# Causal heads of a four-stage layer kernel: products with values in one batch per head instead of two, and 14 places for exponentials instead of 9

## The chip, the cores and the metric

The kernel runs on one core of one Trainium2 chip, as one launch. The metric is the device time of that launch in microseconds; lower is better. Before the change the median of three runs is 1224.54 us (1223.82 to 1226.81).

## The reference

The input `x` has 2 sequences of 1024 tokens with 128 values each. Four stages follow one another, each as `x = layernorm(x + stage(x))`:

```
L0 attention: q, k, v = x W.T + b; 16 heads of 8;  softmax(causal(q k.T / sqrt(8))) v;  W_o
L0 experts:   router, best 2 of 8, relu(x W1 + b1) W2 + b2, weighted sum
L1 attention: q, k through two low-rank factors; 16 heads of 8; causal softmax; W_o
L1 experts:   16 heads of 4 WITHOUT a causal mask, then a router, 8 experts with gelu
```

So there are three attentions. Each has 32 heads (16 heads times 2 sequences), 96 in all. Heads 0 to 31 and 32 to 63 are causal, heads 64 to 95 are not.

## The kernel before, in words

**Two runs.** `RUNS` has heads 0 to 31, followed by 32 units of expert work, and heads 32 to 95, followed by 32 units again. Every engine has its own written-out program over the same loops, and semaphores tie them. Nothing is planned at run time.

**A head.** The scores of a head are made twice. *By query* (`scores_by_query`, line 1195, into three PSUM banks `S1`): VectorE takes row maxima from them (`find_max`, lines 944 and 950). The negated maxima of a head are split in three bf16 parts by GpSimd (`split_max`), turned by TensorE (`max_rows`, line 1218), copied by ScalarE (`rows`, line 828) and sent by a DMA into spare rows of the head's keys and queries. *By key* (`scores_by_key`, line 1210, three PSUM banks `S2`): these come out with the maximum already taken off, and ScalarE writes their exponentials to `probs` (line 851). A causal head has 9 chunks of 512 columns of either sort, since the blocks above the diagonal are left out. Two of the 9 by-query chunks start with a mask product (line 1190); the exponentials of chunks 0 and 5 are masked by GpSimd (line 702). The by-query chunks run two heads ahead of the by-key ones: `head` on TensorE issues by-query chunk c+1 of head g+2 and then by-key chunk c of head g.

**Products with values.** `probs_by_v` (line 1239) multiplies the exponentials (fp32, in `probs`) with a head's values, which stand in 32 columns. A piece is one block of keys against 1 to 4 blocks of queries, and it writes one of four quarters of 32 partitions of the bank `SUM`. `by_key` gives each piece its quarter. Each piece is an fp32 product and shows in the trace as two records. A causal head has 18 pieces, so 36 records. They come in two batches. The batches are `range(0, 5)` and `range(5, 9)` of the chunks. In head g TensorE issues: five pairs of chunks, `max_rows(g + 1)`, **the second batch of head g-1**, a step of other work (`between(at_head(g, 0))`), four pairs of chunks, in every second head `turn_sums`, **the first batch of head g**, and another step of other work (`between(at_head(g, 1))`).

**Places of exponentials.** Chunk c of every causal head goes to place c of 9 in `probs`. ScalarE therefore waits with chunk c of head g until the batch of head g-1 that reads place c is done (`pv_before`, semaphore `pv`).

**A group.** Two causal heads share `SUM`. After the second, ScalarE copies it (`take_sums`, line 833), TensorE turns it (`turn_sums`, line 1249) into the bank `SHARED`, ScalarE takes it out (`take_out`, line 839), GpSimd adds the quarters, and VectorE divides (`normalise`, lines 965 and 967).

**The shared bank.** `SHARED` (bank 7) is used in turn by `max_rows`, `turn_sums` and the steps of other work: transposes, projections, router logits, queries, keys and values of the next attention (lines 1265 to 1327, 1161). `move_in` makes TensorE wait until the last tenant has been taken out. The list `BETWEEN` fixes by hand at which place (head, batch) each step stands. In the causal heads, the steps that use the bank stand after the first of TensorE's stretches, place (g, 0), at heads 13 to 16, 18, 23, 27, 28, 34, 35, 50, 51, 53, 54, 55 and 56. They stand after the second, place (g, 1), at heads 13 to 19, 22, 23, 27, 28, 33, 34, 49, 50, 53, 54, 55 and 56. At even heads `turn_sums` comes before (g, 1).

Of the kernel before, what the change touches and what calls it, by code (L numbers as in the profile page):

```python
# [13 lines left out]
P = 128  # L14
# [5 lines left out]
NH = B * H  # L20
# [3 lines left out]
CH = 512  # L24
# [6 lines left out]
RING = 4  # L31
# [10 lines left out]
class Attention:  # L42


    def __init__(self, layer, head_dim, scale_dim, causal):
        self.layer = layer
        self.hd = head_dim
        self.width = H * head_dim
        self.rows = PARTS * PARTS * head_dim
        self.dv = head_dim + 1  # L50
        self.group = 16 // head_dim
        self.scale = float(scale_dim) ** -0.5
        self.causal = causal
        if causal:

            diagonal = [[(i, i, 1) for i in range(4 * c, 4 * c + 4)] for c in range(2)]
            self.by_query = diagonal + [
                [(7, 0, 4)], [(7, 4, 3), (1, 0, 1)], [(6, 0, 4)], [(6, 4, 2), (2, 0, 2)],
                [(5, 0, 4)], [(5, 4, 1), (3, 0, 3)], [(4, 0, 4)]]
            self.maxima = 3  # L60

            self.by_key = [
                [(i, i, 1, 3) for i in range(4)], [(0, 4, 4, 0)], [(1, 4, 4, 1)], [(2, 4, 4, 2)],
# [3 lines left out]
            self.masked = (0, 5)  # L67
            self.batches = [range(0, 5), range(5, 9)]

            self.pv_order = [  # L70
                [(1, 0), (2, 0), (3, 0), (4, 0), (0, 0), (4, 1), (0, 1), (0, 2), (0, 3)],
                [(6, 0), (8, 0), (7, 0), (8, 1), (5, 1), (5, 0), (7, 1), (5, 2), (5, 3)]]
            self.adds = 3
        else:
            self.by_query = [[(i, 4 * c, 4)] for i in range(TB) for c in range(2)]
            self.maxima = 2
            self.by_key = [[(j, 4 * half, 4, 2 * half + j % 2)] for two in range(0, TB, 2) for half in range(2)
                           for j in range(two, two + 2)]
            self.masked = ()
            self.batches = [range(c, c + 4) for c in range(0, 16, 4)]  # L80
            self.pv_order = [[(c, 0) for c in batch] for batch in self.batches]
            self.adds = 1
        self.chunks = len(self.by_key)

# [7 lines left out]
class Head:  # L92
# [25 lines left out]
            self.key_rows = slice(64 * half, 64 * half + 64)  # L118
            self.max_row = 64 * half + QUERY_ROWS

    def batch_of(self, c):
        return next(k for k, batch in enumerate(self.a.batches) if c in batch)

    def probs_place(self, c):
        return c if self.a.causal else c % 8


HEADS = [Head(g) for g in range(3 * NH)]
RUNS = (range(0, NH), range(NH, 3 * NH))
CHUNKS = [sum(hd.a.chunks for hd in HEADS[:g]) for g in range(3 * NH + 1)]  # L130
BATCHES = [sum(len(hd.a.batches) for hd in HEADS[:g]) for g in range(3 * NH + 1)]
GROUP = [sum(hd.ends_group for hd in HEADS[:g]) for g in range(3 * NH + 1)]
GROUPS = [[hd for hd in HEADS if GROUP[hd.g] == i] for i in range(GROUP[-1])]
ADDS = [sum(heads[0].a.adds for heads in GROUPS[:i]) for i in range(len(GROUPS) + 1)]
# [2 lines left out]
def pv_before(g, c):  # L137

    if not HEADS[g].a.causal and c >= 8:
        return BATCHES[g] + (c - 8) // 4 + 1  # L140
    if g == 0:
        return 0
    if HEADS[g - 1].a.causal:
        return BATCHES[g - 1] + HEADS[g - 1].batch_of(c) + 1
    return BATCHES[g - 1] + (c + 8) // 4 + 1


def queries_upto(run, g, c):
# [172 lines left out]
def build(nc, inp, out):  # L321
    ctx = ExitStack()
    with ctx:
# [20 lines left out]
        qk = sb("qk", [P, RING, 2, S], BF16)  # L344
        v_all = [sb("v8", [P, NH, TB, 9]), sb("v4", [P, NH, TB, 5])]
        v_heads = [sb("v_head8", [P, RING, TB, Q]), sb("v_head4", [P, RING, TB, Q])]
        probs = sb("probs", [P, 9, CH])
        sums = sb("sums", [P, 2, CH])
        by_quarter = sb("by_quarter", [P, 2, 4, 4, 20])
        pairs = sb("pairs", [P, 4, 18])  # L350
# [220 lines left out]
        def _(pool):  # L571
# [81 lines left out]
            def take_v(g):  # L653
                hd = HEADS[g]
                a = hd.a
                ge(pool, "pv", BATCHES[max(g - RING + 1, 0)])
                if a.layer == 0 and hd.n == 0:
                    pool.wait_ge(sem("v_first"), NCH)
                if a.layer > 0 and hd.h == 0:
                    taken(pool, "v", a.layer, BY_SEQUENCE[hd.b][-1])  # L660
                at = a.dv * (hd.n % a.group)
                nc.gpsimd.tensor_copy(v_head_of(a)[:, hd.slot, :, at:at + a.dv], v_of(a)[:, hd.n, :, :]
                                      ).then_inc(sem("v_head"), 1)
# [73 lines left out]
        def _(act):  # L737
# [90 lines left out]
                nc.scalar.activation(neg_rows[:, g % RING, :], neg_ps, ACT.Copy).then_inc(sem("neg_rows"), 1)  # L828

            def take_sums(i):  # L830
                act.wait_ge(sem("pv"), BATCHES[GROUPS[i][-1].g + 1])
                ge(act, "out", i - 1)
                nc.scalar.activation(sums[:, i % 2, :], SUM[:], ACT.Copy).then_inc(sem("sums"), 1)

# [304 lines left out]
        def _(pe):  # L1139
# [81 lines left out]
            def probs_by_v(g, k):  # L1221
                hd = HEADS[g]
                a = hd.a
                order = [(c, b, a.by_key[c][b][1] // 4, a.by_key[c][b][3]) for batch in a.pv_order for c, b in batch]
                opens = {next(m for m in order if m[2:] == hq) for hq in {m[2:] for m in order}}
                closes = {next(m for m in reversed(order) if m[2:] == hq) for hq in {m[2:] for m in order}}
                if k == 0:
                    pe.wait_ge(sem("v_head"), g + 1)
                    if hd.first_of_group:
                        ge(pe, "sums", GROUP[g])  # L1230
                pe.wait_ge(sem("probs"), CHUNKS[g] + a.batches[k][-1] + 1)
                for c, b in a.pv_order[k]:
                    if c in a.masked and (c, b) == next(y for y in a.pv_order[k] if y[0] == c):
                        pe.wait_ge(sem("masked"), 2 * g + a.masked.index(c) + 1)
                    j, q0, count, quarter = a.by_key[c][b]
                    at = P * sum(blk[2] for blk in a.by_key[c][:b])
                    half, q = q0 // 4, P * (q0 % 4)
                    this = (c, b, half, quarter)
                    ins = mm(SUM[Q * quarter:Q * (quarter + 1), q:q + P * count], v_head_of(a)[:, hd.slot, j, :],  # L1239
                             probs[:, hd.probs_place(c), at:at + P * count],  # L1240
                             start=this in opens and hd.first_of_group, stop=this in closes and hd.ends_group,
                             skip_group_check=True)
                ins.then_inc(sem("pv"), 1)
# [87 lines left out]
            def head(run, g, asked):  # L1331
                hd = HEADS[g]
                for k, batch in enumerate(hd.a.batches):
# [11 lines left out]
                        max_rows(g + 1)  # L1345
                    if k == 1 and g > run.start and HEADS[g - 1].ends_group:
                        turn_sums(GROUP[g - 1])
                    if k > 0:
                        probs_by_v(g, k - 1)
                    elif g > run.start:  # L1350
                        probs_by_v(g - 1, len(HEADS[g - 1].a.batches) - 1)
                    if hd.a.causal:
                        between(at_head(g, k))
                return asked
# [35 lines left out]
            for f, run in enumerate(RUNS):  # L1390
# [9 lines left out]
                for g in run:  # L1400
                    asked = head(run, g, asked)
                last = run.stop - 1
                probs_by_v(last, len(HEADS[last].a.batches) - 1)
                experts(f, GROUP[last])


# [68 lines left out]
```

## Time and profile before

| | |
|---|---|
| median of 3 runs | 1224.54 us |
| profiled execution | 1223.02 us, its span 1221.2 us |
| causal heads | about 52 to 308 us and 460 to 735 us of the span |
| experts of the first run | about 308 to 460 us |
| heads 64 to 95 | about 735 to 995 us |
| mean granted TensorE clock | 0.986 of 2.4 GHz |

The page gives each engine's busy time, a strip of 40 slices of 30.5 us each (digits are tenths of busy time), the chain of waits that ended last, and groups of instructions by line. A timeline row gives the start, the time that a merged group covers, engine, line, tile names, shape of the first of them, the count, and in brackets the idle time before it with what ended it. Products on different quarters overlap, so a group's time is far below the sum of its products.

### The profile page before, as it was taken

The numbers are of one execution on the slowest core, as the hardware profiler recorded it, in microseconds if no ns is written. First come the engines' busy times: TensorE is split into PE (matmuls) and PEld (weight loads), VectorE is DVE, ScalarE is ACT, GpSimd is POOL, SyncE is SP. The second block draws the span as 40 slices with busy tenths as digits, with TensorE's granted clock in tenths as the row PEclk, the third lists the DMA queues.
The fourth block names the chain that finished last, engine by engine and source line by source line (L and its number), as shares of the span: only waits on it lengthen the run. The fifth ranks groups of instructions, "written<-read, shape, count | busy, mean of one in ns | idle before, by whom it ended". The sixth has DMA issues, their size and how long they took to land. (4 is left out here: it accounts for less than half of the span.)

```text
span 1221.2 us, 24980 instructions
## 1 busy us (share of the span) xinstructions
PE 1105.6 (91%) x8797; PEld 605.1 (50%) x8872; DVE 864.5 (71%) x2072; ACT 777.3 (64%) x1569; POOL 281.8 (23%) x824
## 2 busy tenths in 40 slices
PE   5899998999999989999988999788888988899996
PEld 3466676655776755666655642222112221137774
DVE  3788767784334467888776889899999989904433
ACT  4366656667444426677666658878888878874443
POOL 8134322333102113433332431111101010100001
PEclk9799999999999999999999999999999989999998
DMA  3444343110000801243312221101111100000000
GB/s 88 118 115 109 96 96 87 49 31 12 1 1 1 184 10 32 59 105 94 85 49 65 55 43 36 24 16 24 36 36 36 23 11 16 7 1 1 10 9 18
DMA packets 40058, 57.71 MB, mean 47 GB/s; under 512 B 9494, under 2 KB 15078, under 8 KB 39678
## 3 DMA queue, kind: packets, MB, share of 16 engines
q1 hardware_dynamic: 39934, 56.11, 18.8%
q8 instruction: 71, 1.16, 0.4%
q14 instruction: 53, 0.43, 0.1%
HBM read 30.81 MB, written 24.64 MB: 45 GB/s over the span
## 5 line engine op out<-in xcount | busy, mean ns | idle before, releaser
L851 ACT ACTIVATE probs<-bank 128x512 f32<-128x512 f32 x1088 | 574.9, 601 | 240.8 <-PE bank L1210 239.8
L950 DVE TENSOR_REDUCE tile_max<-bank 128x1 f32<-128x512 f32 (+3 forms) x1152 | 611.9, 592 | 40.2 <-PE bank L1195 35.6
L1195 PE MATMUL bank<-qk 125*128 125x128 bf16 (+2 forms) x1664 | 389.1, 312 | 66.8 <-DVE tile_max L950 47.0
L1210 PE MATMUL bank<-qk 128*128 128x128 bf16 (+4 forms) x1608 | 362.6, 305 | 5.7 <-ACT probs L851 5.3
L1239 PE MATMUL bank<-probs,v_head 128*32 128x512 f32 (+3 forms) x3328 | 302.9, 453 | 0.1
L1195 PEld LDWEIGHTS bank<-qk 125*128 125x128 bf16 (+1 forms) x1664 | 132.4, 97 | 313.7 <-DVE tile_max L950 243.0
L1117 DVE SCALAR_TENSOR_TENSOR acc<-bank,gate,acc 128x128 f32<-128x128 f32 x256 | 71.9, 343 | 156.7 <-PE bank L1372 156.7
L1239 PEld LDWEIGHTS bank<-probs,v_head 128*32 128x32 f32 x3328 | 139.6, 109 | 52.7 <-issue 29.8
L1210 PEld LDWEIGHTS bank<-qk 128*128 128x128 bf16 (+1 forms) x1664 | 133.1, 97 | 57.2 <-ACT probs L851 21.0
L871 ACT ACTIVATE probs<-bank,sb_b 128x512 f32<-128x512 f32 x128 | 81.0, 684 | 117.9 <-PE bank L1361 117.9
L944 DVE TENSOR_REDUCE tile_max<-bank 128x4 f32<-128x512 f32 x128 | 87.4, 687 | 90.0 <-PE bank L1195 89.9
L1372 PEld LDWEIGHTS bank<-sb_w,probs 128*128 128x128 f32 x1024 | 123.1, 192 | 24.5 <-issue 24.0
L1372 PE MATMUL bank<-sb_w,probs 128*128 128x128 f32 x1024 | 124.7, 275 | 0.0
L1361 PE MATMUL bank<-xT,sb_w 128*128 128x512 f32 x256 | 121.0, 595 | 0.0
L702 POOL TENSOR_SCALAR_AFFINE_SELECT probs<-probs 128x512 f32<-128x512 f32 x128 | 81.6, 638 | 139.3 <-ACT probs L851 139.2
L670 POOL CAST neg_parts<-neg_max 128x8 bf16<-128x8 f32 x96 | 18.5, 193 | 321.7 <-DVE neg_max L957 321.7
L1361 PEld LDWEIGHTS bank<-xT,sb_w 128*128 128x128 f32 x256 | 43.9, 191 | 34.1 <-issue 33.8
L692 POOL TENSOR_TENSOR pairs<-by_quarter 128x72 f32<-128x72 f32 x32 | 11.0, 344 | 161.5 <-ACT by_quarter L839 161.5
L1190 PE MATMUL bank<-mask,ident 128*128 128x512 bf16 x109 | 42.8, 393 | 2.4 <-DVE tile_max L950 1.1
L828 ACT ACTIVATE neg_rows<-bank 24x128 bf16<-24x128 bf16 x96 | 24.7, 257 | 27.1 <-PE bank L1218 27.1
L638 POOL TENSOR_SCALAR rstd<-mean_var 128x4 f32<-128x4 f32 (+1 forms) x12 | 2.9, 238 | 146.2 <-DVE mean_var L1008 146.0
L785 ACT ACTIVATE x<-x_plus,shift,rstd 128x128 f32<-128x128 f32 x64 | 26.2, 487 | 9.8 <-POOL shift L641 9.8
(132 smaller groups left out, 664.2 us busy)
## 6 DMA issues: line engine op xcount, KB each, us to landing
qk<-qk_parts SPq DMA_DIRECT2D x160, 144.0 KB
qk_parts<-q_parts SPq DMA_DIRECT2D x48, 192.0 KB, 2.4
qk_parts<-k_parts SPq DMA_DIRECT2D x48, 192.0 KB, 3.2
qk_parts<-q_parts SPq DMA_DIRECT2D x24, 96.0 KB, 2.3
qk_parts<-k_parts SPq DMA_DIRECT2D x24, 96.0 KB, 2.9
sb_w<-in_w SPq DMA_DIRECT2D x8, 256.0 KB, 3.6
sb_w<-in_w SPq DMA_DIRECT2D x2, 1024.0 KB, 5.2
qk<-neg_rows SPq DMA_DIRECT2D x96, 6.0 KB
```

What stands on the lines that cost most here:

```text
L702: nc.gpsimd.affine_select(out=p, in_=p, compare_op=ALU.is_ge, fill=0.0, base=0, pattern=[[0, 4], [1, P]], channel_multiplier=-1).then_inc( ...
L851: nc.scalar.activation(probs[:, hd.probs_place(c), :], S2[i % len(S2)][:], ACT.Exp, scale=hd.a.scale).then_inc(sem("probs"), 1)
L871: nc.scalar.activation(hidden[:, m % 2, fb, :], bank[2 * (m % 2) + fb][:], ACT.Relu if f == 0 else ACT.Gelu, bias=w_sb[f"b1_{f}"][:, FB * ...
L944: ins = nc.vector.tensor_reduce(tile_max[:, hd.slot, 4 * c:4 * c + 4, 0], s1[:].rearrange("p (t k) -> p t k", k=P), AX.X, ALU.max)
L950: ins = nc.vector.tensor_reduce(tile_max[:, hd.slot, t, which:which + 1], s1[:, at:at + P * count], AX.X, ALU.max)
L1117: ins = nc.vector.scalar_tensor_tensor(acc[:, tile, :], Y[m % 2][:, P * t:P * (t + 1)], gate[:, tile, e:e + 1], acc[:, tile, :], ALU.mult, ...
L1190: mm(s1[:], ident16[:], mask16[:].rearrange("p t k -> p (t k)"), start=True, stop=False, skip_group_check=True)
L1195: ins = mm(s1[:, at:at + P * count], qk[hd.query_rows, hd.place, 0, P * t:P * (t + 1)], qk[hd.query_rows, hd.place, 1, P * k0:P * (k0 + co ...
L1210: ins = mm(s2[:, at:at + P * count], qk[hd.key_rows, hd.place, 1, P * j:P * (j + 1)], qk[hd.key_rows, hd.place, 0, P * q0:P * (q0 + count) ...
L1239: ins = mm(SUM[Q * quarter:Q * (quarter + 1), q:q + P * count], v_head_of(a)[:, hd.slot, j, :], probs[:, hd.probs_place(c), at:at + P * co ...
L1361: ins = mm(bank[2 * (m % 2) + fb][:], w_sb[f"w1_{f}"][:, e, P * fb:P * (fb + 1)], xT[:, tokens(c)], start=True, stop=True)
L1372: ins = mm(Y[m % 2][:, P * t:P * (t + 1)], hidden[:, m % 2, fb, P * t:P * (t + 1)], w_sb[f"w2_{f}"][:, e, fb, :], start=fb == 0, stop=fb = ...
```

## The change

All 18 pieces of a causal head form one batch, in a new written-out order. TensorE issues it in the next head, after that head's first five pairs of chunks, where the second batch stood; the batch after the fourth of the later pairs is gone. The batch waits until all 9 exponentials of its head are there (`probs_upto`). `probs` grows from 9 to 14 places of 512 columns; 9 chunks of a head take the next 9 of the 14 in a ring. Chunks 0 to 4 of head g then wait for the products of head g-2, and chunks 5 to 8 for those of head g-1. `ROUNDS` counts the batches of products in place of `BATCHES`. The chunks, the shared bank, `BETWEEN` and everything of heads 64 to 95 stay, but for the places that head 64 waits for.

```diff
--- before.py
+++ after.py
@@ -68,8 +68,9 @@
             self.batches = [range(0, 5), range(5, 9)]
 
             self.pv_order = [
-                [(1, 0), (2, 0), (3, 0), (4, 0), (0, 0), (4, 1), (0, 1), (0, 2), (0, 3)],
-                [(6, 0), (8, 0), (7, 0), (8, 1), (5, 1), (5, 0), (7, 1), (5, 2), (5, 3)]]
+                [(1, 0), (2, 0), (3, 0), (4, 0), (0, 0), (0, 1), (6, 0), (8, 0), (8, 1), (0, 2), (5, 1), (0, 3),
+                 (5, 2), (7, 0), (5, 0), (5, 3), (4, 1), (7, 1)]]
+            self.probs_upto = [9]
             self.adds = 3
         else:
             self.by_query = [[(i, 4 * c, 4)] for i in range(TB) for c in range(2)]
@@ -79,6 +80,7 @@
             self.masked = ()
             self.batches = [range(c, c + 4) for c in range(0, 16, 4)]
             self.pv_order = [[(c, 0) for c in batch] for batch in self.batches]
+            self.probs_upto = [4, 8, 12, 16]
             self.adds = 1
         self.chunks = len(self.by_key)
 
@@ -118,17 +120,14 @@
             self.key_rows = slice(64 * half, 64 * half + 64)
             self.max_row = 64 * half + QUERY_ROWS
 
-    def batch_of(self, c):
-        return next(k for k, batch in enumerate(self.a.batches) if c in batch)
-
     def probs_place(self, c):
-        return c if self.a.causal else c % 8
+        return (9 * (self.g - 2 * NH) + c) % 14 if self.a.causal else c % 8
 
 
 HEADS = [Head(g) for g in range(3 * NH)]
 RUNS = (range(0, NH), range(NH, 3 * NH))
 CHUNKS = [sum(hd.a.chunks for hd in HEADS[:g]) for g in range(3 * NH + 1)]
-BATCHES = [sum(len(hd.a.batches) for hd in HEADS[:g]) for g in range(3 * NH + 1)]
+ROUNDS = [sum(len(hd.a.pv_order) for hd in HEADS[:g]) for g in range(3 * NH + 1)]
 GROUP = [sum(hd.ends_group for hd in HEADS[:g]) for g in range(3 * NH + 1)]
 GROUPS = [[hd for hd in HEADS if GROUP[hd.g] == i] for i in range(GROUP[-1])]
 ADDS = [sum(heads[0].a.adds for heads in GROUPS[:i]) for i in range(len(GROUPS) + 1)]
@@ -137,12 +136,14 @@
 def pv_before(g, c):
 
     if not HEADS[g].a.causal and c >= 8:
-        return BATCHES[g] + (c - 8) // 4 + 1
+        return ROUNDS[g] + (c - 8) // 4 + 1
     if g == 0:
         return 0
+    if HEADS[g].a.causal:
+        return ROUNDS[g - 1] if c < 5 else ROUNDS[g]
     if HEADS[g - 1].a.causal:
-        return BATCHES[g - 1] + HEADS[g - 1].batch_of(c) + 1
-    return BATCHES[g - 1] + (c + 8) // 4 + 1
+        return ROUNDS[g - 1] if c < 4 else ROUNDS[g]
+    return ROUNDS[g - 1] + (c + 8) // 4 + 1
 
 
 def queries_upto(run, g, c):
@@ -344,7 +345,7 @@
         qk = sb("qk", [P, RING, 2, S], BF16)
         v_all = [sb("v8", [P, NH, TB, 9]), sb("v4", [P, NH, TB, 5])]
         v_heads = [sb("v_head8", [P, RING, TB, Q]), sb("v_head4", [P, RING, TB, Q])]
-        probs = sb("probs", [P, 9, CH])
+        probs = sb("probs", [P, 14, CH])
         sums = sb("sums", [P, 2, CH])
         by_quarter = sb("by_quarter", [P, 2, 4, 4, 20])
         pairs = sb("pairs", [P, 4, 18])
@@ -653,7 +654,7 @@
             def take_v(g):
                 hd = HEADS[g]
                 a = hd.a
-                ge(pool, "pv", BATCHES[max(g - RING + 1, 0)])
+                ge(pool, "pv", ROUNDS[max(g - RING + 1, 0)])
                 if a.layer == 0 and hd.n == 0:
                     pool.wait_ge(sem("v_first"), NCH)
                 if a.layer > 0 and hd.h == 0:
@@ -828,7 +829,7 @@
                 nc.scalar.activation(neg_rows[:, g % RING, :], neg_ps, ACT.Copy).then_inc(sem("neg_rows"), 1)
 
             def take_sums(i):
-                act.wait_ge(sem("pv"), BATCHES[GROUPS[i][-1].g + 1])
+                act.wait_ge(sem("pv"), ROUNDS[GROUPS[i][-1].g + 1])
                 ge(act, "out", i - 1)
                 nc.scalar.activation(sums[:, i % 2, :], SUM[:], ACT.Copy).then_inc(sem("sums"), 1)
 
@@ -1228,7 +1229,7 @@
                     pe.wait_ge(sem("v_head"), g + 1)
                     if hd.first_of_group:
                         ge(pe, "sums", GROUP[g])
-                pe.wait_ge(sem("probs"), CHUNKS[g] + a.batches[k][-1] + 1)
+                pe.wait_ge(sem("probs"), CHUNKS[g] + a.probs_upto[k])
                 for c, b in a.pv_order[k]:
                     if c in a.masked and (c, b) == next(y for y in a.pv_order[k] if y[0] == c):
                         pe.wait_ge(sem("masked"), 2 * g + a.masked.index(c) + 1)
@@ -1345,10 +1346,10 @@
                         max_rows(g + 1)
                     if k == 1 and g > run.start and HEADS[g - 1].ends_group:
                         turn_sums(GROUP[g - 1])
-                    if k > 0:
+                    if k == 0 and g > run.start:
+                        probs_by_v(g - 1, len(HEADS[g - 1].a.pv_order) - 1)
+                    if k > 0 and not hd.a.causal:
                         probs_by_v(g, k - 1)
-                    elif g > run.start:
-                        probs_by_v(g - 1, len(HEADS[g - 1].a.batches) - 1)
                     if hd.a.causal:
                         between(at_head(g, k))
                 return asked
@@ -1400,7 +1401,7 @@
                 for g in run:
                     asked = head(run, g, asked)
                 last = run.stop - 1
-                probs_by_v(last, len(HEADS[last].a.batches) - 1)
+                probs_by_v(last, len(HEADS[last].a.pv_order) - 1)
                 experts(f, GROUP[last])
```

## Rows read from the trace of the kernel before

**Rows 1.** The page, parts 1 and 2: busy time, and its tenths in 40 slices.

```profile
PE 1105.6 (91%) x8797; PEld 605.1 (50%) x8872; DVE 864.5 (71%) x2072; ACT 777.3 (64%) x1569; POOL 281.8 (23%) x824
...
PE   5899998999999989999988999788888988899996
```

**Rows 2.** Window, length; busy PE, PEld, DVE, ACT, POOL (count); clock; DMA share; GB/s.

```profile
52.00:305.00 253.00, 239.86 (x2440) 160.00 (x2475) 186.72 (x459) 167.49 (x363) 87.31 (x267) 1.00 0.30 77
464.00:734.00 270.00, 251.52 (x2439) 157.83 (x2471) 211.91 (x493) 177.50 (x372) 94.84 (x283) 0.99 0.26 66
```

**Rows 3.** Timeline of TensorE in heads 11 and 12.

```profile
131.59 0.39 PE L1195 MATMUL bank<-qk 125*128 125x512 bf16 x1
...
132.62 0.39 PE L1195 MATMUL bank<-qk 125*128 125x512 bf16 x1 [0.19 <-DVE tile_max L950]
...
133.75 0.38 PE L1210 MATMUL bank<-qk 128*128 128x384 bf16 x2
134.06 1.51 PE L1239 MATMUL bank<-probs,v_head 128*32 128x512 f32 x18
135.51 0.39 PE L1190 MATMUL bank<-mask,ident 128*128 128x512 bf16 x1
...
135.96 0.39 PE L1210 MATMUL bank<-qk 128*128 128x128 bf16 x4
...
138.06 1.07 PE L1239 MATMUL bank<-probs,v_head 128*32 128x384 f32 x18
139.06 0.39 PE L1195 MATMUL bank<-qk 125*128 125x512 bf16 x1
...
141.06 0.60 PE L1249 MATMUL bank<-ident,sums 128*128 128x128 f32 x4
141.59 1.51 PE L1239 MATMUL bank<-probs,v_head 128*32 128x512 f32 x18
```

**Rows 4.** Timeline of TensorE, the end of head 31.

```profile
305.23 2.38 PE L1239 MATMUL bank<-probs,v_head 128*32 128x512 f32 x36
307.54 1.12 PE L1361 MATMUL bank<-xT,sb_w 128*128 128x512 f32 x2
```

**Rows 5.** Timeline of VectorE, the same stretch as rows 3.

```profile
131.15 0.25 DVE L965 RECIPROCAL den_inv<-total 128x16 f32<-128x16 f32 x1
...
131.82 2.60 DVE L950 TENSOR_REDUCE tile_max<-bank 128x1 f32<-128x256 f32 x6
...
136.16 0.69 DVE L944 TENSOR_REDUCE tile_max<-bank 128x4 f32<-128x512 f32 x1 [0.93 <-PE bank L1195]
```

**Rows 6.** All engines around turn_sums of head 14.

```profile
159.44 1.51 PE L1239 MATMUL bank<-probs,v_head 128*32 128x512 f32 x18
159.60 0.43 ACT L839 ACTIVATE by_quarter<-bank 128x288 f32<-128x288 f32 x1
```

**Rows 7.** All engines at place (18, 0).

```profile
191.17 1.07 PE L1239 MATMUL bank<-probs,v_head 128*32 128x384 f32 x18
192.32 0.26 ACT L828 ACTIVATE neg_rows<-bank 24x128 bf16<-24x128 bf16 x1
...
192.73 0.63 PE L1265 MATMUL bank<-ident,a_tok 128*128 128x128 f32 x4 [0.48 <-ACT neg_rows L828]
```

**Rows 8.** Timeline of TensorE at place (23, 0).

```profile
238.47 0.63 PE L1285 MATMUL bank<-ident,x 128*128 128x128 f32 x4 [2.01 <-ACT neg_rows L828]
```

**Rows 9.** All engines at place (33, 1).

```profile
472.03 1.64 ACT L785 ACTIVATE x<-x_plus,shift,rstd 128x128 f32<-128x128 f32 x4
...
472.49 1.51 PE L1239 MATMUL bank<-probs,v_head 128*32 128x512 f32 x18
```

**Rows 10.** Timeline of VectorE while the heads turn non-causal.

```profile
716.69 3.68 DVE L950 TENSOR_REDUCE tile_max<-bank 128x1 f32<-128x512 f32 x6 [0.39 <-PE bank L1195]
```

**Rows 11.** Timeline of the DMA queue, the same stretch as rows 3.

```profile
131.60 0.78 SPq L506 DMA_DIRECT2D qk<-neg_rows  x1
```

**Rows 12.** The page, part 6: issues, KB each, us to landing.

```profile
qk_parts<-q_parts SPq DMA_DIRECT2D x48, 192.0 KB, 2.4
```

## The prediction, made before the changed kernel was run

> **What bounds the kernel now.** I read the page first, then the two causal stretches, then single heads on each engine. TensorE is busy 91% of the span and nearly full in all causal slices [rows 1]. In the causal stretches it is busy 240 of 253 us and 252 of 270 us; VectorE has 187 and 212, ScalarE 167 and 178 [rows 2]. VectorE and ScalarE wait for TensorE once per head: VectorE for 0.93 us in head 12's turn [rows 5]. So TensorE is the bound of the causal heads, and its time per head counts. Head 11 takes 7.47 us (131.59 to 139.06) [rows 3].
>
> The reader is to follow the parts of a head in [rows 3]. A by-query or by-key chunk or a mask product takes 0.22 us from start to start: two of them lie between 135.51 and 135.96. A head has 20 of them, 4.4 us. The second batch of products (36 records in two batches, 18 here) takes 1.00 us to the next chunk, 138.06 to 139.06; the first batch takes 1.45 us, 134.06 to 135.51. Before the first batch stands a short break: the last by-key chunk starts at 133.75, its 512 columns need 0.22, and the batch starts at 134.06, 0.09 later. Last, in odd heads TensorE waits for VectorE in the four-pair stretch: 131.59 to 134.06 is 2.47, of which nine items take 1.98 and the break 0.09, so 0.40 is waiting; the one bracket of it shows 0.19 at 132.62. (In heads 39 to 59 the same stretch is 0.2 shorter.) VectorE comes late there because it divides (131.15 to 131.82) ahead of its chunks [rows 5]. Even heads have `turn_sums` (141.06 to 141.59) and no such wait.
>
> **One batch in place of two.** A piece's length in units of 128 columns, summed per quarter, is the length of a batch. In the first batch the fullest quarters have 6 units, in the second 4. The times 1.45 and 1.00 give 0.22 per unit and 0.11 fixed. All 18 pieces fill the quarters with 10, 10, 8 and 8 units, so one batch is 10 x 0.22 + 0.11 = 2.32 us. The trace has this very case: at the end of head 31 both batches stand together, and 36 records take 2.31 us until the next product [rows 4]. Against 1.45 + 1.00 that saves 0.14. The break before the first batch goes too, 0.09. Together 0.23 per head, and 63 pairs of batches are merged (head 31's were together already): **-14.5 us**. Bounds: 0.09 per head (5.7 us) if the new order packs worse, 0.35 (22 us) if `turn_sums` loses its own break as well.
>
> Here a rule of the Trainium skill is to be weighed. The row is the 1.45 us of the first batch, 6 units and 0.11 [rows 3]. The page TensorE: Matmul & The Clock Gate, Part 3 (Packing small matmuls), says that matmuls keep strict program order, and that only weight loads are pulled ahead. With whole pieces starting in program order the first batch would have 7 units, because `(4, 1)` waits for quarter 0 while three pieces of quarter 3 stand behind it; the second would have 5, and the new order 10. The merge would then save two units more. With 7 and 5 units the fixed part would be -0.09 us, which cannot be, so the trace speaks against it; what it would give is the last rival.
>
> **Places and waits of ScalarE.** With 14 places chunks 0 to 4 wait for head g-2's products, which are done a whole head before. Chunks 5 to 8 wait for head g-1's, as before, and their scores stand behind that batch on TensorE anyway. Cost 0; bounds 0 to 0.1 us per head. `probs_upto` waits for all 9 exponentials of a head behind five further pairs: 0. The mask of chunk 5 has those five pairs too, on GpSimd, which is busy 87 of 253 us [rows 2]: 0.
>
> **The feed of VectorE.** Its 4 chunks q5, q6, q7, q8 took 2.60 us in 6 instructions [rows 5], 0.65 each, and a pair costs TensorE only 0.45. TensorE may be 3 banks ahead. Now a pause of 1.45 lets VectorE catch up after four pairs and one of 1.00 after five. Then it is nine pairs in a row and a pause of 2.31. I follow a head: VectorE starts 0.4 us after the batch, and reaches its fifth chunk at about 3.0, sixth 3.6, seventh 4.2. TensorE wants the banks of the sixth and seventh 0.2 us before each is free, about 0.34 us in all in odd heads; the 0.53 of `turn_sums` covers it in even heads. The wait after the division goes in exchange, since VectorE has 2.31 us for it. So 0.34 against 0.2 to 0.4: **0**. Bounds: -0.3 and +0.3 us in each of the 32 odd heads, -10 to +10 us.
>
> **Who has to wait for the maxima.** The copy of the negated maxima follows the same exponential, and its DMA is issued at 131.60 and used by head 12's first by-key chunk at 135.96, with no wait there [rows 3, 11]. In the new order that use is about 0.45 us earlier, 3.9 us after the issue starts. The issue takes 0.78 [rows 11]; the nearest transfer with a time lands in 2.4 us [rows 12] and is 32 times larger, so 3.2 at most: 0. Without that cover each head would lose up to its shortage. The loads of heads are issued and needed at the same distance as before.
>
> **Steps after the one batch, places (g, 0).** These steps wait until ScalarE has copied the maxima out of the shared bank. The second batch covered 0.93 us of this; the new one covers 2.31. At (18, 0) the batch starts at 191.17, so it ends at 192.10 (0.93 later, the 1.00 less the tail), and the step starts at 192.73: 0.63 lost [rows 7]. At (23, 0) 2.01 us are shown as waited, since four normalisations stand ahead on ScalarE; 2.15 with the edge [rows 8]. Read so at all 16 places: five have 0.63, five about 0.29, four about 0.08, (23, 0) 2.15 and (53, 0) 1.3, in all 8.4. A longer cover of 1.3 takes all but 0.8 of it: **-7.6 us**.
>
> **Steps after the four pairs, places (g, 1).** Here the first batch was the cover, and it is gone. In even heads `turn_sums` has just filled the shared bank. ScalarE takes it out from 159.60 to 160.03, while the batch runs from 159.44 [rows 6]; a step needs another 0.15 us to start (192.58 to 192.73 at place (18, 0)) [rows 7]. Without the batch TensorE stands for 0.72 us. That is the case at nine heads (14, 16, 18, 22, 28, 34, 50, 54, 56): 6.5 us, and 0.3 more at 22, where ScalarE is late. In odd heads the last step at (g, 0) has mostly been taken out in time, but not the normalised rows: at head 33 ScalarE works on them from 472.03 to 473.67, the step could start at 472.49, and so 1.3 us are lost [rows 9]. Head 53 is alike (1.45), and 23 and 27 lose 0.3 each. Together **+10.1 us**. Bounds: +6 (a stall here lets VectorE catch up, and removes its waits later) and +16 (each stall also shifts ScalarE's next copy).
>
> **Ends.** In heads 30 and 31 no by-query chunks are left and ScalarE is nearly the bound; it has work for about 1.8 us during a pause of 2.3 + 0.3: +0.5 to 0.8 in each, +1.0 in all. In heads 61 to 63 two by-query chunks go with each pair, and VectorE is the bound, idle 0.39 at a pause of 1.00 [rows 10]. With 2.31 it is idle 1.7, against 1.0 to 1.4 for its two pauses now: +0.4 each, **+2.2 us** with the former. Bounds 0 and +5.
>
> **Sum.** -14.5 - 7.6 + 10.1 + 2.2 = -9.8 us. The profiled execution took 1223.0 us, its span 1221.2, so 1213.2; the median of the runs shown lies 1.5 above that execution. I take **1214 us**.
>
> **Rivals.**
> - *The feed decides in both kinds of head.* Three banks do not carry nine pairs, and TensorE waits 0.25 us more in every head. For it: VectorE needs 0.65 where TensorE needs 0.45. Against it: VectorE still has about 1 us idle per head. 63 x 0.25 = 15.8 us are lost, which gives 1230; at half that price, the likelier size, **1222**.
> - *The feed gets better.* The division falls wholly under the pause and the later waits do not come: 32 x 0.3 us more, **1204**. For it: the steps fill many odd heads and remove these waits. Against it: my walk through the banks.
> - *The shared bank decides, on the other side.* The mechanism is a step at (g, 1) behind a bank that ScalarE has not emptied, with ScalarE's normalisations and copies ahead. I have 13 such places at 0.78 on average; the kernel becomes slower from 1.5 us each. At the 2.0 us of [rows 8] it is 26 instead of 10.1 us, and the time is **1230**. Against it: ScalarE reaches its copy 0.16 us after `turn_sums` [rows 6].
> - *Pieces in program order*, as the page has it. Then two more units, 0.44 us, go in each head, 28 us: **1186**.
> - *The merge does not do what it says*: the new order packs worse than that of [rows 4], and takes 2.45. Then 63 x 0.14 = 8.8 us are not won: **1223**.
>
> **How the numbers follow.** My forecast has 0.57 (its own range 1208 to 1219), the better feed 0.14, the worse feed 0.12, the worse packing 0.04, the shared bank 0.10, program order 0.02, 0.01 for none of these. Faster by over 0.3% (3.7 us; less cannot be told from no change) means below 1220.9: 0.77. Within: 0.13. Slower: 0.10. The range 1203 to 1222 leaves out half of the better feed, the slow rival, program order, and the tails of the feed.
>
> **What would show it.** In the changed trace one group of 36 records in each causal head, 2.3 us from start to next chunk; if 2.45 or 1.9, the first step is wrong. Plain heads of about 7.1 us (odd) and 7.3 (even) in place of 7.47 and 7.53. Step by step: the waits for the maxima's copy at (g, 0) gone but at head 23; new waits of TensorE for `by_quarter` at the nine even heads, 0.7 us each; waits for normalised rows at heads 33 and 53. If VectorE's share in TensorE's waits doubles, the feed was mis-sized. If the heads without steps do not get shorter, the forecast is wrong as a whole.

## The result, and the profile after

The changed kernel takes **1249.01 us** (median of 4 runs, 1247.51 to 1251.05) against 1224.18 before: a ratio of 1.0202, 95% interval 1.0187 to 1.0217. It is 2% slower. I had forecast 1214, range 1203 to 1222. The profiled execution has a span of 1247.4 us.

Busy time and its tenths, as in [rows 1], and the causal stretches, as in [rows 2] (these stretches are now 10 and 18 us longer):

```profile
PE 1110.7 (89%) x8806; PEld 602.8 (48%) x8872; DVE 865.4 (69%) x2072; ACT 787.8 (63%) x1569; POOL 280.2 (22%) x824
...
PE   5899998989999988999978998888888988899996
```

```profile
52.00:315.00 263.00, 241.61 (x2478) 159.64 (x2511) 187.07 (x460) 173.82 (x366) 87.26 (x267) 1.00 0.28 74
472.00:760.00 288.00, 257.30 (x2467) 158.94 (x2496) 214.70 (x495) 185.13 (x377) 94.27 (x283) 0.98 0.25 62
```

TensorE has nearly the same busy time (1110.7 against 1105.6 us) in a span 26.2 us longer. VectorE's busy time is the same; ScalarE's is 10.5 us more, though its 1088 exponentials still take 601 to 602 ns each. So most of the added time is TensorE waiting.

TensorE in two plain heads, the counterpart of [rows 3]:

```profile
124.36 2.37 PE L1240 MATMUL bank<-probs,v_head 128*32 128x512 f32 x36
126.67 0.39 PE L1196 MATMUL bank<-qk 125*128 125x512 bf16 x1
...
128.66 0.61 PE L1250 MATMUL bank<-ident,sums 128*128 128x128 f32 x4
129.10 0.38 PE L1191 MATMUL bank<-mask,ident 128*128 128x512 bf16 x1
...
132.37 0.23 PE L1219 MATMUL bank<-ident,neg_parts 128*24 128x128 bf16 x1 [0.65 <-POOL neg_parts L678]
132.47 2.38 PE L1240 MATMUL bank<-probs,v_head 128*32 128x512 f32 x36
134.78 0.39 PE L1196 MATMUL bank<-qk 125*128 125x512 bf16 x1
...
137.43 0.38 PE L1196 MATMUL bank<-qk 125*128 125x512 bf16 x1
137.65 0.38 PE L1211 MATMUL bank<-qk 128*128 128x512 bf16 x1
138.03 0.39 PE L1196 MATMUL bank<-qk 125*128 125x384 bf16 x2
138.25 0.38 PE L1211 MATMUL bank<-qk 128*128 128x512 bf16 x1
138.62 0.39 PE L1196 MATMUL bank<-qk 125*128 125x512 bf16 x1
138.85 0.38 PE L1211 MATMUL bank<-qk 128*128 128x512 bf16 x1
139.22 0.39 PE L1196 MATMUL bank<-qk 125*128 125x256 bf16 x2
...
139.76 0.23 PE L1219 MATMUL bank<-ident,neg_parts 128*24 128x128 bf16 x1
...
142.07 0.39 PE L1196 MATMUL bank<-qk 125*128 125x512 bf16 x1
```

The batch is what I had said: 36 records, 2.31 us from 132.47 to 134.78. An odd head (134.78 to 142.07) takes 7.29 us. The even head takes 8.11 (126.67 to 134.78), and the row at 132.37 tells why: `max_rows` waits, 0.65 by its bracket, and what ended it is L678, **GpSimd's last step of splitting the maxima**. Nothing waited there in a plain head before. GpSimd and ScalarE just before:

```profile
129.35 0.41 ACT L840 ACTIVATE by_quarter<-bank 128x288 f32<-128x288 f32 x1
```

```profile
129.84 0.34 POOL L693 TENSOR_TENSOR pairs<-by_quarter 128x72 f32<-128x72 f32 x1 [5.95 <-ACT by_quarter L840]
130.26 0.33 POOL L695 TENSOR_TENSOR total<-pairs,by_quarter 128x72 f32<-128x72 f32 x1
130.53 0.25 POOL L697 COPY total<-by_quarter 128x72 f32<-128x72 f32 x1
130.72 0.64 POOL L703 TENSOR_SCALAR_AFFINE_SELECT probs<-probs 128x512 f32<-128x512 f32 x1
131.30 0.19 POOL L671 CAST neg_parts<-neg_max 128x8 bf16<-128x8 f32 x1
131.58 0.20 POOL L673 TENSOR_TENSOR neg_rest<-neg_max,neg_parts 128x8 f32<-128x8 f32 x1
131.84 0.19 POOL L676 CAST neg_parts<-neg_rest 128x8 bf16<-128x8 f32 x1
132.11 0.20 POOL L678 TENSOR_TENSOR neg_parts<-neg_rest,neg_parts 128x8 bf16<-128x8 f32 x1
```

The reader is to see one queue, back to back, from 129.84 to 132.31: three sums of quarters, the mask of chunk 5, four steps of `split_max`. It starts when ScalarE has taken the turned sums out of the bank. From that take-out's start to `max_rows` are 3.02 us. In the kernel before the same two events were 3.83 us apart, and the split stood ready 0.84 us before use, because the first batch lay between `turn_sums` and the five pairs:

```profile
141.75 0.42 ACT L839 ACTIVATE by_quarter<-bank 128x288 f32<-128x288 f32 x1
```

```profile
144.53 0.20 POOL L677 TENSOR_TENSOR neg_parts<-neg_rest,neg_parts 128x8 bf16<-128x8 f32 x1
```

```profile
145.58 0.23 PE L1218 MATMUL bank<-ident,neg_parts 128*24 128x128 bf16 x1
```

The change removed that batch, 1.44 us, from the distance.

What TensorE waited for, over the whole span; columns: total us, times, longest:

```profile
PE bank L1219 <- POOL neg_parts L678: 15.4, 18, 3.4
...
PE bank L1191 <- DVE tile_max L951: 6.2, 8, 1.8
```

Before, these were:

```profile
PE bank L1218 <- POOL neg_parts L677: 2.3, 3, 2.0
...
PE bank L1190 <- DVE tile_max L950: 1.1, 3, 0.6
```

The brackets count only idle time beyond the modelled end of the product before, so each real wait is some 0.15 us longer (0.65 in the bracket at 132.37, 0.81 between the two lengths of an even head, 8.11 here and 7.30 in e1 below).

Where the delay against the kernel before arises, read from the starts of the 96 `max_rows`: heads 2 to 31 +6.3 us, the end of the first run +2.4, heads 32 to 62 +10.1, heads 62 to 66 +5.5, and later +2.6, at stretches of the lower clock; 26.9 in all, where the spans differ by 26.2.

### The profile page after: what moved, and what is told of

Its sections match the earlier page's. It is cut to its first block and busy times, and to the rows that moved or that the text cites. A ratio compares the mean times of both kernels' runs of the same rounds, so it can differ in the third digit from the quotient of the medians.

```text
span 1247.4 us, 24984 instructions
## 1 busy us (share of the span) xinstructions
PE 1110.7 (89%) x8806; PEld 602.8 (48%) x8872; DVE 865.4 (69%) x2072; ACT 787.8 (63%) x1569; POOL 280.2 (22%) x824
## 3 DMA queue, kind: packets, MB, share of 16 engines
q8 instruction: 71, 1.16, 0.4%
## 5 line engine op out<-in xcount | busy, mean ns | idle before, releaser
L852 ACT ACTIVATE probs<-bank 128x512 f32<-128x512 f32 x1088 | 580.9, 602 | 210.8 <-PE bank L1211 208.4
L1240 PE MATMUL bank<-probs,v_head 128*32 128x128 f32 (+3 forms) x3328 | 295.0, 458 | 1.3 <-ACT probs L852 1.2
L1240 PEld LDWEIGHTS bank<-probs,v_head 128*32 128x32 f32 x3328 | 136.2, 110 | 54.4 <-issue 25.4
L703 POOL TENSOR_SCALAR_AFFINE_SELECT probs<-probs 128x512 f32<-128x512 f32 x128 | 81.3, 635 | 127.9 <-ACT probs L852 127.2
L945 DVE TENSOR_REDUCE tile_max<-bank 128x4 f32<-128x512 f32 x128 | 83.7, 684 | 30.3 <-PE bank L1196 30.2
L834 ACT ACTIVATE sums<-bank 128x512 f32<-128x512 f32 x40 | 23.9, 596 | 50.2 <-PE bank L1240 46.3
L1191 PE MATMUL bank<-mask,ident 128*128 128x512 bf16 x126 | 48.9, 388 | 6.5 <-DVE tile_max L951 6.2
L1219 PE MATMUL bank<-ident,neg_parts 128*24 128x128 bf16 x96 | 21.9, 228 | 17.9 <-POOL neg_parts L678 15.4
```

Source lines behind the costliest of these rows:

```text
L703: nc.gpsimd.affine_select(out=p, in_=p, compare_op=ALU.is_ge, fill=0.0, base=0, pattern=[[0, 4], [1, P]], channel_multiplier=-1).then_inc( ...
L852: nc.scalar.activation(probs[:, hd.probs_place(c), :], S2[i % len(S2)][:], ACT.Exp, scale=hd.a.scale).then_inc(sem("probs"), 1)
L945: ins = nc.vector.tensor_reduce(tile_max[:, hd.slot, 4 * c:4 * c + 4, 0], s1[:].rearrange("p (t k) -> p t k", k=P), AX.X, ALU.max)
L1191: mm(s1[:], ident16[:], mask16[:].rearrange("p t k -> p (t k)"), start=True, stop=False, skip_group_check=True)
```

## The experiments

Runs of the kernel before beside these gave medians of 1223.6 to 1223.9 us. A ratio is to it.

**e1, GpSimd splits first.** The changed kernel, with this in GpSimd's `head`, so that in causal heads the quarters are added after the split:

```diff
                 for k in range(len(hd.a.batches)):
-                    if k == 1 and g > run.start and HEADS[g - 1].ends_group:
+                    if k == 1 and g > run.start and HEADS[g - 1].ends_group and not hd.a.causal:
                         add_quarters(GROUP[g - 1])
 ...
                 if g + AHEAD < run.stop:
                     split_max(g + AHEAD)
+                if g > run.start and HEADS[g - 1].ends_group and hd.a.causal:
+                    add_quarters(GROUP[g - 1])
```

> The changed kernel, but in causal heads GpSimd splits the maxima (split_max) before it adds the quarters of a finished group (add_quarters). Theory G: with the later batch gone, turn_sums comes too shortly before max_rows of the next head; GpSimd's queue (add quarters, mask, split: 3.0 us from the take-out of the bank to the turned maxima) is longer than the five pairs that lie between, so each even head waits 0.8 us. Then even plain heads go from 8.1 to 7.3 us and the time falls by the 21 us that the weight loads of L1219 waited for GpSimd, to about 1228 (1224 to 1233). Theory F: VectorE cannot be fed through nine pairs, and the waits on GpSimd only take its place: then TensorE waits for VectorE instead and the time stays at 1245 to 1250.

Measured: 1230.05 us, 1.0047 (1.0030 to 1.0064). 19 us go, so most of the loss hangs on the order in GpSimd's queue. Plain even heads take 7.30 us:

```profile
124.48 0.61 PE L1252 MATMUL bank<-ident,sums 128*128 128x128 f32 x4
...
127.48 0.23 PE L1221 MATMUL bank<-ident,neg_parts 128*24 128x128 bf16 x1
127.49 2.37 PE L1242 MATMUL bank<-probs,v_head 128*32 128x512 f32 x36
129.79 0.39 PE L1198 MATMUL bank<-qk 125*128 125x512 bf16 x1
...
134.78 2.37 PE L1242 MATMUL bank<-probs,v_head 128*32 128x512 f32 x36
```

From `turn_sums` (124.48) to `max_rows` (127.48) nothing is idle now, and the next head follows at the same 7.30.

**e2, the same swap in the kernel before.**

> Control: the kernel before with the same swap on GpSimd. Theory G: the kernel before has 0.8 us between the split maxima and their use in even heads, so nothing waits and nothing is won: 1224, within 2 us. If the swap alone gave 5 us or more, then e1 would not speak of the change.

Measured: 1221.02 us, 0.9974 (0.9964 to 0.9984). 3 us are won, not within 2 us of 1224: the kernel before had a wait for GpSimd of its own at one head with normalisations, around head 54 (2.9 us by the starts of `max_rows`). Plain heads take 7.53 and 7.3 to 7.4. The expectation missed by about 1 us; 5 us or more would have spoken against e1. So 3 of e1's 19 us are not of the change, and 16 are.

**e3 and e4, a dose.** One more select on GpSimd ahead of `split_max` in even heads:

```diff
+                if hd.a.causal and g > run.start and HEADS[g - 1].ends_group:
+                    link(nc.gpsimd.affine_select(out=spare[:], in_=mask16[:], compare_op=ALU.is_ge, fill=0.0, ...))
                 if g + AHEAD < run.stop:
                     split_max(g + AHEAD)
```

> The changed kernel with one more select of 128x512 on GpSimd (0.64 us by L703) ahead of split_max in each of the 31 even or run-opening causal heads that have a finished group before them. Theory G: this queue has no slack in even heads, so nearly all of it is paid: +0.64 x 24 to 30 heads = +15 to +19 us, 1264 to 1268. Theory F: the queue has slack that VectorE's lateness makes: 1249 to 1252.

> The kernel before with the same extra select. Theory G: 0.84 us of slack in plain even heads covers 0.64, so 1224 to 1228. If GpSimd mattered in the kernel before as well, it would be +15 us.

Measured: e3 1259.64 us, 1.0289 (1.0272 to 1.0306), 10.6 above the changed kernel; e4 1227.01, 1.0033 (1.0020 to 1.0047), 3.4 above the kernel before. In e3 every plain even head pays 0.82 us (8.01 to 8.83 between `max_rows`): the select takes 0.70 from its start to the next step's, and a cast of the split behind it 0.30 in place of 0.19. The total is below the 15 to 19 us expected: heads 14 to 20, with steps of other work, pay nothing in the starts of `max_rows`, so their chain had slack. In e4 the plain heads of the second run pay nothing, 7.30 and 7.53, but for one of 8.16. What e4 pays in the first run has another cause, told at the end.

**e5, the turn earlier.** GpSimd's order as in the changed kernel; `turn_sums` and `take_out` behind chunk 6 instead of chunk 8, in the even heads with no bank step at (g, 0):

```diff
+                        if c == 6 and early(run, g):
+                            take_out(GROUP[g - 1])
 ...
-                    if k == 1 and group_done:
+                    if k == 1 and group_done and not early(run, g):
 ...
+                        if c == 6 and early(run, g):
+                            turn_sums(GROUP[g - 1])
 ...
-                    if k == 1 and g > run.start and HEADS[g - 1].ends_group:
+                    if k == 1 and g > run.start and HEADS[g - 1].ends_group and not early(run, g):
```

> The changed kernel, GpSimd's order as it is, but in the even heads with no bank step at (g, 0) turn_sums and take_out come after the pair of chunk 6 in place of chunk 8. Theory G: the take-out comes 0.9 us earlier, so add_quarters and then split_max do, and the 0.8 us wait of about 20 plain even heads goes without touching GpSimd's order: 1232 to 1236. Rival: split_max is late because VectorE's maxima are late; then the order on the bank changes nothing, 1248 to 1251.

Measured: 1233.98 us, 1.0084 (1.0068 to 1.0099). The other end of the same chain gives the same cure, 15 us: plain even heads take 7.35 us.

**e6, 14 places alone.** The kernel before with `(9 * (self.g - 2 * NH) + c) % 14` and the waits that belong to it, two batches.

> The kernel before, two batches, with only the 14 places (and the waits that belong to them). Theory G: the places are neither gain nor loss, 1224 within 2 us. Rival: ScalarE's freer start or other bank addresses of the exponentials move the time by over 4 us.

Measured: 1222.47 us, 1.0000 (0.9983 to 1.0016). No gain, no loss. Its heads start `max_rows` 0.7 to 1.3 us ahead of the kernel before through all 96, so they keep its pace.

**e9, the order of the pieces.**

```diff
-                [(1, 0), (2, 0), (3, 0), (4, 0), (0, 0), (0, 1), (6, 0), (8, 0), (8, 1), (0, 2), (5, 1), (0, 3),
-                 (5, 2), (7, 0), (5, 0), (5, 3), (4, 1), (7, 1)]]
+                [(1, 0), (2, 0), (3, 0), (4, 0), (0, 0), (4, 1), (0, 1), (0, 2), (0, 3),
+                 (6, 0), (8, 0), (7, 0), (8, 1), (5, 1), (5, 0), (7, 1), (5, 2), (5, 3)]]
```

> The changed kernel with the 18 pieces in the order of the two old batches, one behind the other. If the quarters run on their own, 10 units decide in either order: the batch takes 2.31 us as now and the time is that of the changed kernel, 1249 within 2 us. If pieces start in program order, this order has 12 units where the new one has 10: 0.43 us more in each head, 1276.

Measured: 1248.09 us, 1.0198 (1.0180 to 1.0216), that of the changed kernel. The new order is neither better nor worse:

```profile
131.40 2.38 PE L1240 MATMUL bank<-probs,v_head 128*32 128x512 f32 x36
133.71 0.39 PE L1196 MATMUL bank<-qk 125*128 125x512 bf16 x1
```

131.40 to 133.71 is the same 2.31 us.

**e7 and e8, the old two batches where the long one is in the way.** A head in a list `SPLIT` keeps its two batches, with places and waits in the ring of 14; e7 lists heads 30, 31, 61, 62, 63, and e8 also 14, 16, 18, 28, 33, 34, 50, 53, 54, 56. Both have e1's swap.

```diff
+    @property
+    def pv_order(self):
+        return SPLIT_ORDER if self.split() else self.a.pv_order
 ...
-                    if k > 0 and not hd.a.causal:
+                    if k > 0 and (hd.split() or not hd.a.causal):
                         probs_by_v(g, k - 1)
```

> e1 with the old two batches in heads 30, 31, 61, 62 and 63 alone. In e1 the delay against the kernel before grows by 2.4 us between heads 31 and 32 and by 5 us between heads 61 and 66; the theory is that there ScalarE (first) and VectorE (second) are the bound and idle through the long batch. Then 6 to 8 us go: 1222 to 1224. Rival: these losses come from elsewhere (clock stretches, the experts' start), and the time stays within 2 us of e1's 1230.

> e7 with the old two batches also in heads 14, 16, 18, 28, 33, 34, 50, 53, 54 and 56, where a step at (g, 1) lost its cover. By the prediction's own prices (0.72 us at an even head, 1.3 and 1.45 at heads 33 and 53, less 0.23 for the merge and less the waits that come back at the next (g, 0)) 4 us go against e7: 1218 to 1220. Rival: the waits at (g, 1) let VectorE catch up and cost nothing in the end: as e7.

Measured: e7 1224.09 us, 1.0010 (0.9996 to 1.0024), 6 less than e1; e8 1220.04, 0.9971 (0.9961 to 0.9982), 4 less than e7, at the upper edge of what was expected. e7's eleven runs lie in two groups, six from 1222.05 to 1224.09 and five from 1226.86 to 1228.80; the profiled one is of the second. In the starts of `max_rows` e7 gains 1.8 us on e1 at heads 31 to 35 and 3.8 at heads 62 to 66, 5.6 together, and e8 gains 4.3 on e7 at the heads that it adds. What the long batch does at the end of the second causal run stands in the changed kernel's trace, on VectorE, then on TensorE:

```profile
738.13 3.68 DVE L951 TENSOR_REDUCE tile_max<-bank 128x1 f32<-128x512 f32 x6 [3.22 <-PE bank L1196]
...
751.30 3.68 DVE L951 TENSOR_REDUCE tile_max<-bank 128x1 f32<-128x512 f32 x6 [2.81 <-PE bank L1196]
```

```profile
734.48 3.29 PE L1240 MATMUL bank<-probs,v_head 128*32 128x512 f32 x36
```

VectorE, the bound there, stands for 3.22 and 2.81 us (0.39 in [rows 10]). Two things add up: three banks last VectorE 1.8 us (0.61 each, six chunks in 3.68), and the granted clock was at its lower level, 1.2 GHz, for two stretches of 3.4 us right there (from 732.97 and from 746.62), so that the batch took 3.22 us (734.48 to 737.70) in place of 2.31. From 718.50 to 733.00 before them TensorE is shown busy for 13.09 of 14.50 us, every other by-query chunk held up for VectorE by 0.17 to 0.21 us. The kernel before had no such stretch at these heads; e7 has none there either, but two of 3.4 us in heads 68 to 70, which took 2.5 us back. So the clock's part is not settled to better than 2 us.

**e10, less work for VectorE.** In `find_max` `for t, first, count in a.by_query[c][:1]`, so three of the nine chunks' second maxima are left out.

> e1 with the second maximum of the three by-query chunks that cover two query tiles left out (VectorE reads only the first piece of chunks 3, 5 and 7), so VectorE has about 1.0 us less per head. Feed theory: in e1 odd heads still hold three waits of TensorE for VectorE, 0.46 us in all, and even heads none, since turn_sums covers them. Then odd heads go from 7.30 to 6.85 us, even ones stay, and with the steps' heads and the ends the time falls 9 to 13 us, to 1217 to 1221. Rival: the odd heads' 0.46 is something else on TensorE (exponentials, or a fixed gap), and the time stays within 3 us of 1230.

Measured: 1213.35 us, 0.9909 (0.9893 to 0.9925), 17 us below e1. Plain odd heads 6.92 us, even ones 7.28:

```profile
115.46 0.23 PE L1221 MATMUL bank<-ident,neg_parts 128*24 128x128 bf16 x1
...
122.74 0.23 PE L1221 MATMUL bank<-ident,neg_parts 128*24 128x128 bf16 x1
...
129.66 0.23 PE L1221 MATMUL bank<-ident,neg_parts 128*24 128x128 bf16 x1
```

From 122.74 to 129.66 is the odd head. It lost 0.38 of the 0.46; the even one kept its 7.3. So VectorE's lateness is the odd heads' wait. The total is 4 us below the 1217 to 1221 expected. By the starts of `max_rows`, 13 plain odd heads make 4.9 us of the difference to e1, the openings of the two runs (heads 0 to 2 and 31 to 35) 6.3, the stretches around heads 21, 25, 36 and 52 together 2.3, and heads 13 to 20 nothing.

**e11, odd heads in two batches.** As e8, with all odd causal heads in `SPLIT`, so 22 even heads are left merged.

> e8 with the old two batches also in all odd causal heads, so that only plain even heads are merged. Feed theory: the odd head's first batch after four pairs gives VectorE its pause back (0.46 us of waits go) and costs 0.23: a plain pair of heads takes 14.4 in place of 14.6 us, the time 1215 to 1218. Rival: the even head's nine pairs behind a batch of only 1.0 us starve VectorE in their turn, and the time is that of e8 (1220) or up to 3 us more.

Measured: **1215.60 us, 0.9932 (0.9916 to 0.9947)**, faster than both kernels. A pair of plain heads takes 14.38 us (120.99 to 135.37):

```profile
120.99 0.39 PE L1213 MATMUL bank<-qk 125*128 125x512 bf16 x1
...
125.99 2.37 PE L1257 MATMUL bank<-probs,v_head 128*32 128x512 f32 x36
...
130.37 1.51 PE L1257 MATMUL bank<-probs,v_head 128*32 128x512 f32 x18
131.81 0.39 PE L1208 MATMUL bank<-mask,ident 128*128 128x512 bf16 x1
...
134.36 1.07 PE L1257 MATMUL bank<-probs,v_head 128*32 128x384 f32 x18
135.37 0.39 PE L1213 MATMUL bank<-qk 125*128 125x512 bf16 x1
```

The even head's long batch (125.99) is followed by four pairs, the odd head's first batch (130.37), five pairs and its second (134.36). Of the 8 us that it wins, e2's swap alone gives 3.

## Why the prediction was wrong

**The batch: right.** 2.31 us in place of 1.45 + 1.00, in either order (e9); the rival of program order, which would have made e9 27 us longer, and the one of worse packing fall. (10 x 0.22 + 0.11 is 2.31, not the 2.32 written.) In plain even heads with GpSimd out of the way the saving is the 0.23 that I had: 7.53 to 7.30.

**The places: right.** e6 gives 0.

**"Who has to wait for the maxima": the step that failed.** I followed the copy of the maxima and its DMA behind `max_rows`, and priced that at 0. I did not ask what `max_rows` itself waits for. It is the split on GpSimd, and that engine's queue has `add_quarters` ahead of it, which waits for `turn_sums`. I had counted the removed first batch as cover for a step at (g, 1), and saw that the turned bank is taken out late; the same take-out opens GpSimd's queue, 3.0 us long, and 2.3 were left for it (in e1 3.00 from `turn_sums` to `max_rows`, less the 0.69 from `turn_sums` to the take-out). Price: 1247.4 to 1228.1 in the spans, **19 us** (e1, and 15 by the other end of the chain, e5). The kernel before loses 3 of these to the same queue (e2), so **16 us** of the 35 between forecast and result are this step's. The dose shows that no slack was left in even plain heads, and that before there was enough for one more select of 0.70 (e3, e4); the rows put it at 0.84.

**"The feed of VectorE": mis-sized.** I had 0.34 us in odd heads for 0.2 to 0.4 before, so 0. It was three waits of 0.15 to 0.16 us, 0.46 in all: in the changed kernel's odd head the chunks at 138.03, 138.62 and 139.22 start 0.37 to 0.38 behind the one before, in place of the 0.22 between 137.43 and 137.65. So plain odd heads took 7.3 us where I had announced 7.1. In e1 a plain pair of heads won 0.37 us in the first run and 0.23 in the second, where I had 0.46: some 5 us, if all 32 pairs are counted like the plain ones. And TensorE's waits for VectorE before a mask product went from 1.1 to 6.2 us, nearly all of it in five waits around heads 21, 25, 33, 36 and 52. e10 took 2.4 us out of these five; that waits for others had hidden the rest before is my reading and not shown. e10 cut VectorE's busy time by 58.5 us (865.2 to 806.7) and won 17, so VectorE's lateness costs real time; my rival of the worse feed was a part of the result, beside another that I had not named.

**Steps after the long batch (g, 0): right as far as it goes.** The waits for the copied maxima are gone but for 0.4 us. These waits gave back 5.4 us by the brackets, and TensorE's waits for VectorE's maxima grew by 4.8 over the span. At heads 13 to 20, however, e10 with less work for VectorE takes as long as e1, so there it is not shown that VectorE took the gain.

**Steps at (g, 1): right.** TensorE waits nine times for `by_quarter`, 0.5 to 0.66 us by the brackets, at the steps of even heads, and 1.16 and 1.64 us for the normalised rows at heads 33 and 53. Giving ten of these heads their cover back won 4.05 us where my prices gave 4 (e8); the two groups of e7's runs make so close a match partly luck, but the starts give 4.3.

**Ends: too small.** I had 2.2 us; e7 measures 6 in the medians, 5.6 in the starts. At the end of the first run I left out that all 18 products now wait for the last exponential (TensorE stood 1.17 us there, and 18 of them ran before it in the kernel before); at the end of the second VectorE's idle time was 2.8 to 3.2 us at a batch, where I had 1.7.

**The sum.** -9.8 forecast, +16 GpSimd (19 less the 3 that the kernel before loses too), +5 VectorE in plain pairs, +5 VectorE at steps, +4 the ends: +20, where the span grew by 26.2. Of the 6 left, 2.6 lie behind head 66 at changes of the clock; they were not tried by themselves, and the rest stays open.

**The slow rival** had the right sign and the wrong place: I had looked for a late bank on ScalarE with 13 places, and the late one was GpSimd's queue behind it, in every second head.

## What to carry to other kernels

Before a piece of work is taken out of the bound engine's stream, list what every later wait of that stream depends on, through all engines, and the time from each one's start to its use; the work that goes was part of that distance. A wait that never shows may have 0.8 us of slack, and a change that takes 1.4 us turns it into a loss in each turn of the loop. And look at the engine that the bound one feeds on: here VectorE was 78% and 84% as busy as TensorE in the two causal stretches [rows 2], with three buffers between them, and in odd heads two short pauses were worth more than one long one (e11). The fastest version here that leaves no work out merges only where a further item of the bound engine (the turn) already gives the other its pause.

## What was not expected of the hardware

VectorE's division can be held by a GpSimd operation. In e4 the extra select moved GpSimd's 1.27 us sum for the residual (L629) onto it:

```profile
117.27 1.27 POOL L629 TENSOR_TENSOR x_plus<-x,sb_bo 128x512 f32<-128x512 f32 x1
```

```profile
117.55 1.14 DVE L971 TENSOR_TENSOR a_tok<-total,den_inv 128x128 f32<-128x128 f32 x1
118.61 2.60 DVE L954 TENSOR_REDUCE tile_max<-bank 128x1 f32<-128x256 f32 x6
```

The division of 128x128 (L971) took 1.14 us in place of 0.29. GpSimd's sum began first and ended at 118.54, the division at 118.69, 0.15 later; TensorE then waited 0.65 us by its bracket for VectorE. That is most of what e4 pays: four plain odd heads of the first run go from 7.47 to 8.16 us. In e1 a division of 0.95 us (128.33 to 129.28) also ended 0.15 behind such a sum (127.84 to 129.13), and in the kernel before the one between the rows of [rows 5] did as well (sum from 130.47 to 131.75):

```profile
131.44 0.46 DVE L967 TENSOR_TENSOR a_tok<-total,den_inv 128x128 f32<-128x128 f32 x1
```

In the changed kernel fifteen divisions take 0.53 to 0.54 us, each beside a select of GpSimd's (L703) that began first; that at 132.51 ends at 133.04, the select at 132.90. The reductions, which read a bank, kept their 0.65 us per chunk beside GpSimd's work (in the kernel before three chunks in 1.94 us from 129.30, with GpSimd at work throughout). Over all 40 divisions the mean was 317 ns before and 386 in the changed kernel, 2.8 us more in all; no run took this away by itself.

The Trainium skill, SBUF — State Buffer, section Who interferes with whom, says that VectorE and GpSimd share one pair of ports under an exclusive lock, so that the later of two operations waits for the whole of the earlier one; its rules for kernel authors name a VectorE operation with two inputs in SBUF against a GpSimd operation that reads SBUF. The division has two such inputs, and its four times here (0.46, 0.53, 0.95 and 1.14 us) agree with that.
